# A language-model tower's front block: the embedding product moves two slots ahead and to the end of a step, the second-layer products next to the first, and ScalarE writes the rows of the second norm

## The reference, cut to what matters

```python
h = tok(x, emb_2, emb_3, emb_4)            # 64 x 256 tokens, 64 wide: three gathered rows, summed, / 4
h = h + attn(layernorm(h), k_w1, k_w2, q_w1, q_w2, v_w)
#   phase = tanh(tanh(x w1 + b1) w2 + b2) * pi, for keys and for queries (32 phases each)
#   out[t] = sum over t' <= t of (cos, sin)(key phase of t') . (cos, sin)(query phase of t) * value[t'] / norm[t]
h = h + experts(layernorm(h), edge_index)  # graph attention over 262,144 edges picks two of four experts
h = h + attn_of_heads(layernorm(h))
h = h + mlp_of_half_the_tokens(layernorm(h))
```

## Time and profile before

| what | us |
|---|---|
| median of 3 runs (lowest, highest) | 3619.52 (3614.86, 3619.73) |
| the profiled execution, its own time | 3614.07 |
| its span, first to last instruction | 3612.3 |
| VectorE busy in the span | 2905.8 |
| TensorE busy | 2745.7 |
| GpSimd busy | 2357.0 |
| ScalarE busy | 2233.4 |

### The profile page before, as it was taken

How to read it: one execution, slowest core, us unless ns; L and a number is a source line. 1 busy time by engine, 2 the same in 40 slices (tenths; PEclk the granted TensorE clock), 3 DMA queues, 4 the chain that set the end, 5 groups by cost and what they waited for, 6 DMA issues and landing times. The chain is left out here.

```text
span 3612.3 us, 65404 instructions
## 1 busy us (share of the span) xinstructions
PE 2745.7 (76%) x21085; PEld 2339.2 (65%) x21085; DVE 2905.8 (80%) x5994; ACT 2233.4 (62%) x3840; POOL 2357.0 (65%) x2290
## 2 busy tenths in 40 slices
PE   2556665649999999999999999999999500077747
PEld 1445554438888888888888888888888400054436
DVE  9988878847888888888888888888888857777764
ACT  2555545558787777777777777777777112255523
POOL 7887877027777777777777777777777577233311
PEclk8666667759999999999999999999999855566669
DMA  2111111012222222222222222222221132000002
GB/s 73 22 23 25 24 24 21 5 47 48 49 49 49 49 49 49 49 49 49 49 49 49 49 49 49 49 49 49 49 49 41 21 101 77 26 0 0 0 0 47
DMA packets 157459, 144.94 MB, mean 40 GB/s; under 512 B 71192, under 2 KB 133032, under 8 KB 156728
## 3 DMA queue, kind: packets, MB, share of 16 engines
q1 hardware_dynamic: 88608, 109.56, 9.1%
q0 software_dynamic: 68768, 34.45, 8.8%
HBM read 93.03 MB, written 50.82 MB: 40 GB/s over the span
## 5 line engine op out<-in xcount | busy, mean ns | idle before, releaser
L886 POOL DMA_INDIRECT es_got<-node_table,late x1632 | 1577.6, 967 | 497.3 <-issue 497.3
L966 PE MATMUL es_pgot<-hash_space,es_pick 128*128 128x256 bf16 x13056 | 1510.3, 277 | 16.4 <-ACT es_pick L904 16.4
L966 PEld LDWEIGHTS es_pgot<-hash_space,es_pick 128*128 128x128 bf16 x13056 | 1300.0, 100 | 182.6 <-issue 16.9
L900 ACT ACTIVATE es_pick<-es_away,consts 128x512 bf16<-128x512 f32 x1088 | 680.3, 712 | 7.0 <-DMA es_away<-sorted_keys 6.7
L348 POOL DMA_INDIRECT fr_ring<-in_emb,fr_rows x384 | 498.7, 1299 | 138.9 <-issue 115.8
L904 ACT ACTIVATE es_pick<-es_pick,consts 128x4096 bf16<-128x4096 bf16 x136 | 503.8, 3704 | 0.9
L1068 DVE TENSOR_TENSOR es_hot<-es_iota,late 128x1024 bf16<-128x1024 f32 x272 | 331.8, 1220 | 26.7 <-DVE es_st L1108 25.7
L1069 DVE TENSOR_TENSOR es_hot<-es_iota,late 128x1024 bf16<-128x1024 f32 x272 | 330.5, 1215 | 0.0
L1050 DVE TENSOR_REDUCE es_got<-es_prod 128x32 f32<-128x512 f32 x272 | 277.2, 1019 | 39.6
L1048 DVE TENSOR_TENSOR es_prod<-es_pgot,es_own 128x512 f32<-128x512 f32 x272 | 187.5, 689 | 123.4 <-PE es_pgot L966 86.2
L932 ACT ACT_TABLE_LOAD x64 | 82.1, 1283 | 301.2 <-PE ex_phid L973 301.2
(11 more groups left out here) (345 smaller groups left out, 4316.2 us busy)
## 6 DMA issues: line engine op xcount, KB each, us to landing
es_away<-sorted_keys SPq DMA_DIRECT2D x68, 512.0 KB
es_got<-node_table,late POOLq DMA_INDIRECT x1632
edge_states<-es_st SPq DMA_DIRECT2D x68, 384.0 KB, 2.4
expert_outputs<-ex_y SPq DMA_DIRECT2D x64, 256.0 KB
gt_y<-expert_outputs SPq DMA_DIRECT2D x8, 2048.0 KB, 8.6
fr_ring<-in_emb,fr_rows POOLq DMA_INDIRECT x384, 2.5
out_dram<-h SPq DMA_DIRECT2D x1, 4096.0 KB, 16.0
weights<-in_weights SPq DMA_DIRECT2D x1, 2110.0 KB, 14.0
```

The lines of the kernel that those rows point to most:

```text
L886: pool.indirect_dma_start(out=got[:, r, k, :], out_offset=None, in_=table_dram, in_offset=bass.IndirectOffsetOnAxis(ap=src[:, n, k:k + 1]. ...
L900: a.activation(pick[:, r, half, k], away[:, r, half * 4 * P:half * 4 * P + 4 * P], ACT.Square, bias=C("away")[:, k:k + 1]).then_inc(s_act, 1)
L966: mm = pe.matmul(p_got[:, q, c * 256:c * 256 + 256], pick[:, r, q // 2, k, at * P:at * P + P], parts[:, part, k], start=(k == 0 and part = ...
```

## The change

Five edits, all in `front`:

1. The embedding product is made two slots ahead, as the last thing of a step on TensorE (`embed(s + 2)`), and ScalarE evicts and squares it as the last thing of its step. Slot 1 is made in step 0.
2. The second-layer products (L774 before) follow the first-layer ones with only the table product and a possible turn between.
3. Of the second norm VectorE computes only the reciprocal and the product of mean and reciprocal (a 128 x 4 operation); ScalarE writes the four rows (an activation with scale and bias taken per partition).
4. Constants of placing: `turn_at` of the later parts of a step are called with t + 3.8 and t + 4.5 where they were t + 3.6, t + 4.2 and t + 5.0, and while a turn is under way, VectorE may pull a part forward by 1.3 exchanges where it was 0.8.
5. The last steps are fewer by one: slots 30 and 31 pass the second norm together.

```diff
--- before.py
+++ after.py
@@ -300,7 +300,12 @@
         PHASES = [("k", top) for top in range(1, 19)] + [("k", 18), ("t", 14)]
         final, final_top = (sum(range(1, 19)) + 1 + 18) % 2, 14 % 2
         is_slot = lambda s: 0 <= s < SLOTS
-        STEPS = SLOTS + 3
+        STEPS = SLOTS + 2
+
+        def lasts(s):
+
+            return [s - 3] if 3 <= s <= SLOTS else [SLOTS - 2, SLOTS - 1] if s == SLOTS + 1 else []
+
         top_dram = mem["top_dram"]
 
         stage = ExitStack()
@@ -381,13 +386,22 @@
             def root(s, ln):
                 a.activation(std[:, ln, slot(s)], var[:, ln, slot(s)], ACT.Sqrt, scale=1.0 / D, bias=C("eps")).then_inc((s_std0, s_std1)[ln], 1)
 
+            def normed(s, ln):
+
+                act.wait_ge((s_near0, s_near1)[ln], s + 1)
+                for t in range(ST):
+                    col = slice(s * ST + t, s * ST + t + 1)
+                    to = x1[:, t] if ln else x0[:, t % 2, t // 2]
+                    ins = a.activation(to, h[:, s * ST + t], ACT.Identity, scale=std[:, ln, col], bias=away[:, ln, col])
+                ins.then_inc((s_x0, s_x1)[ln], 1)
+
             evict(0)
             squares(0, 0)
             root(0, 0)
             one_set()
             act.wait_ge(s_weights, 16)
             for s in range(STEPS):
-                before, last = s - 1, s - 3
+                before = s - 1
                 if is_slot(before):
                     act.wait_ge(s_fold, before + 1)
 
@@ -395,28 +409,30 @@
                 if is_slot(s):
                     act.wait_ge(s_xt_p, s + 1)
                     a.activation(xt[:], p_xt, ACT.Copy).then_inc(s_xt, 1)
-                if is_slot(last):
+                for last in lasts(s):
+                    normed(last, 1)
                     act.wait_ge(s_x1_p, last + 1)
                     a.activation(xts[:, last * 2:last * 2 + 2], p_x1.rearrange("p (t n) -> p t n", t=2), ACT.Copy).then_inc(s_x1t, 1)
+                    if not is_slot(s):
+                        act.wait_ge(s_tab_p, last + 1)
+                        a.activation(tab[:, slot(last)], p_tab.rearrange("p (t r) -> p t r", r=ROW), ACT.Copy).then_inc(s_tab, 1)
                 if is_slot(s):
                     act.wait_ge(s_hid_p, s * 2 + 2)
                     for kq in range(2):
                         a.activation(hid[:, kq], p_hid[:, kq], ACT.Tanh, bias=W("q_b1" if kq else "k_b1")).then_inc(s_hid, 1)
-                if is_slot(s + 1):
-                    evict(s + 1)
-                    squares(s + 1, 0)
-                if is_slot(last):
-                    act.wait_ge(s_tab_p, last + 1)
-                    a.activation(tab[:, slot(last)], p_tab.rearrange("p (t r) -> p t r", r=ROW), ACT.Copy).then_inc(s_tab, 1)
-                if is_slot(s):
+                    for last in lasts(s):
+                        act.wait_ge(s_tab_p, last + 1)
+                        a.activation(tab[:, slot(last)], p_tab.rearrange("p (t r) -> p t r", r=ROW), ACT.Copy).then_inc(s_tab, 1)
                     act.wait_ge(s_ph, s * 2 + 2)
                     for kq in range(2):
                         a.activation(u[:, kq], p_ph[:, kq], ACT.Tanh, bias=W("q_b2" if kq else "k_b2")).then_inc(s_u, 1)
-                if is_slot(s + 1):
-                    root(s + 1, 0)
-                if is_slot(s - 2):
-                    root(s - 2, 1)
-                if is_slot(s):
+                    if s == 0:
+                        evict(1)
+                        squares(1, 0)
+                    if is_slot(s + 1):
+                        root(s + 1, 0)
+                    if is_slot(s - 2):
+                        root(s - 2, 1)
                     one_set()
                 if is_slot(before):
                     act.wait_ge(s_out, before + 1)
@@ -426,9 +442,15 @@
                             ins.then_inc(s_res, 1)
                     act.wait_ge(s_res, before + 1)
                     squares(before, 1)
+                if s == SLOTS:
+                    root(SLOTS - 2, 1)
+                    root(SLOTS - 1, 1)
                 if is_slot(s):
                     act.wait_ge(s_v, s + 1)
                     a.activation(val[:].rearrange("p two b d -> p (two b d)"), p_v, ACT.Copy).then_inc(s_val, 1)
+                if is_slot(s + 2):
+                    evict(s + 2)
+                    squares(s + 2, 0)
 
         @block.vector
         def _(dve):
@@ -487,11 +509,13 @@
 
                 dve.wait_ge((s_std0, s_std1)[ln], s + 1)
                 ch.step(v.reciprocal(std[:, ln, slot(s)], std[:, ln, slot(s)])); ch.settle()
-                for t in range(ST):
-                    col = slice(s * ST + t, s * ST + t + 1)
-                    to = x1[:, t] if ln else x0[:, t % 2, t // 2]
-                    ins = v.tensor_scalar(to, h[:, s * ST + t], away[:, ln, col], std[:, ln, col], ALU.add, ALU.mult)
-                ins.then_inc((s_x0, s_x1)[ln], 1)
+                if ln:
+                    v.tensor_tensor(away[:, ln, slot(s)], away[:, ln, slot(s)], std[:, ln, slot(s)], ALU.mult).then_inc(s_near1, 1)
+                else:
+                    for t in range(ST):
+                        col = slice(s * ST + t, s * ST + t + 1)
+                        ins = v.tensor_scalar(x0[:, t % 2, t // 2], h[:, s * ST + t], away[:, ln, col], std[:, ln, col], ALU.add, ALU.mult)
+                    ins.then_inc(s_x0, 1)
 
             def split(j):
 
@@ -510,8 +534,8 @@
                 if part == 0:
                     if is_slot(s):
                         normed(s, 0)
-                    if is_slot(s - 3):
-                        normed(s - 3, 1)
+                    for last in lasts(s):
+                        normed(last, 1)
                 if part == 1:
                     if is_slot(s - 1):
                         for b in range(SB):
@@ -559,7 +583,7 @@
                 turns[0] += 1
                 dve.sem_inc(s_turn_go, 1)
                 if arr == "k":
-                    between(done[0] + 0.8)
+                    between(done[0] + 1.3)
                 dve.wait_ge(s_turned, turns[0])
                 return turned[:, 0:COLS if arr == "k" else P]
 
@@ -656,7 +680,7 @@
                 s, part = divmod(at[0], 3)
                 attention(s, part)
                 at[0] += 1
-                if s >= SLOTS - 1 and ready < 3 and part != 1:
+                if s == SLOTS and part < 2:
                     prepare(ready)
                     ready += 1
             while ready < 3:
@@ -717,10 +741,18 @@
                                        ring[:, r, n].rearrange("p (b two) d -> p two b d", two=2)[:, half], start=(n == 0), stop=(n == 2))
                 mm.then_inc(s_emb, 1)
 
+            def table(s):
+
+                pe.wait_ge(s_x1t, s + 1)
+                pe.wait_ge(s_wx, 1)
+                for two in range(2):
+                    mm = pe.matmul(p_tab[:, two * 2 * ROW:two * 2 * ROW + 2 * ROW], xts[:, s * 2 + two], wx[:].rearrange("p two r -> p (two r)"), start=True, stop=True)
+                mm.then_inc(s_tab_p, 1)
+
             embed(0)
             pe.wait_ge(s_weights, 16)
             for s in range(STEPS):
-                before, last = s - 1, s - 3
+                before = s - 1
                 t = step_time(s)
                 turn_at(t + 0.1)
                 if is_slot(s):
@@ -737,15 +769,17 @@
                         k, q = (phi[b * D:b * D + D, kq] for kq in range(2))
                         pe.matmul(p_sc[b][:, 0:256], k[:, 0:P], q, start=True, stop=True)
                         pe.matmul(p_sc[b][:, 256:384], k[:, P:T], q[:, P:T], start=True, stop=True).then_inc(s_sc, 1)
-                if is_slot(last):
+                for last in lasts(s):
                     pe.wait_ge(s_x1, last + 1)
                     if is_slot(s):
                         pe.wait_ge(s_xt, s + 1)
-                    elif last >= 1:
+                    else:
                         pe.wait_ge(s_tab, last)
                     for two in range(2):
                         mm = pe.transpose(p_x1[:, two * P:two * P + P], x1[:, 2 * two:2 * two + 2].rearrange("p two d -> p (two d)"), ident)
                     mm.then_inc(s_x1_p, 1)
+                    if not is_slot(s):
+                        table(last)
                 if is_slot(before):
                     if before >= 1:
                         pe.wait_ge(s_res, before)
@@ -759,20 +793,15 @@
                     for kq in range(2):
                         pe.matmul(p_hid[:, kq], W("q_w1" if kq else "k_w1"), xt[:], start=True, stop=True).then_inc(s_hid_p, 1)
                 turn_at(t + 2.9)
-                if is_slot(s + 1):
-                    embed(s + 1)
-                if is_slot(last):
-                    pe.wait_ge(s_x1t, last + 1)
-                    pe.wait_ge(s_wx, 1)
-                    for two in range(2):
```

(13 more changed lines are left out.)

4 lines of the change are left out of this document (2 added, 2 removed).

## The result

The changed kernel took 3589.48 us, median of 5 runs (3585.23 to 3600.26), against 3617.19 for the kernel before in the same session: ratio 0.993, 95% interval 0.9918 to 0.9942. I had forecast 3613, no change that can be told, with 3595 as the lower end. The profiled execution took 3585.23 us, 28.8 less than the one before; my sum had 6.5 less.

What follows compares the result with a forecast made beforehand. VectorE's work or waiting was taken to bound the front after 222 us, with gathers alongside before. -16.6 - 41.5 + 15 + 30 + 5 + 1.6 = -6.5 us, so 3613 us as a median, range 3595 to 3627.

Steps and rivals of the forecast that it cites:

- There both walk together: First stretch, before 222 us: GpSimd's gathers (20.3 us a slot) and VectorE's seven steps (144.3 us) keep one pace.
- Rows of the second norm: Middle stretch: VectorE spared 0.72 us a step over 23 steps, -16.6 us; ScalarE's four rows, 1.1 us, cost nothing.
- Second layer: Middle stretch: VectorE's 35.0 us of waits for the second tanh and 6.5 for scores go, -41.5 us.
- ring: Dependence loop from mask through products, tanh, eviction, squares, sine and scores to mask: 18.3 us binds six short steps, +15 us.
- Turns and embedding product: Steps 8, 10 lose 7 and 5 us; 15, 27, 29 lose 16 together; with smaller terms, +30 us.
- Two slots ahead: First stretch: mask of slot 0 moves from 77.75 to 88.4, of slot 7 to 227; +5 us, bounds 0 and 8.
- the end: Last chain of the front: slots 30 and 31 add two writings of rows and drop some waiting, +1.6 us.
- Rival 1: The gain stays: faster TensorE, turns cost +12, ring 17 us and +7; -32 us, 3587. Chance 0.20.
- Rival 2: Slower by turns alone: slow TensorE after idling costs seven step-end turns 2 us more each, +14; 3627. Chance 0.15.
- Rival 3: The wait only moves: first-layer product held back 0.8 us, short steps cost 5 more; sum -1, 3618. Chance 0.20.

Runs made afterwards that it cites:

- the kernel with both parts: Kernel before plus ScalarE's second-norm rows and second-layer products next to the first, embedding product one slot ahead behind them: 3567.00 us, ratio 0.9858; disturbed 0.9967 and 0.9963.
- disturbed groups: Four of six groups of runs, in which TensorE paused with nothing to wait for and every kernel, the one before too, took 5260 to 5336 us.

## Why the prediction was wrong

Most of its mechanisms held. One did not, and left a part of the gain at nothing; several sizes were off as well. The sum was 22.4 us too high: 5.4 in the first stretch, 12.5 in the middle, 1.2 at the end, and 3.2 behind the front block, which the change doesn't touch.

**"There both walk together", the first stretch, is the step whose mechanism failed.** I took GpSimd's gathers as a limit beside VectorE and so counted neither the rows nor the second layer there, only the second slot's +5. The runs show -6.5 for the rows, -6.8 for the second layer, -11.6 for both (222.0 to 210.5), and +11.2 for the rest of the change. For the rows, the gathers gave way with VectorE's work: from the start of slot 3's to the end of slot 9's they took 141.5 us before and 133.9 with the rows on ScalarE. For the second layer they did not (140.5 us), and the seven steps were 6.8 us shorter all the same: before, the gathers were no limit any more by the end of the stretch. The last gather of slot 8 and the embedding product of slot 8, before:

```profile
197.23 0.94 POOL L348 DMA_INDIRECT fr_ring<-in_emb,fr_rows  x1 [0.30 <-issue]
...
201.80 2.04 PE L760 MATMUL fr_pb<-fr_xt,weights 128*128 128x256 f32 x4 [0.77 <-DVE fr_sm L519]
203.64 2.16 PE L716 MATMUL fr_turned<-fr_ring,consts 128*128 128x128 f32 x12
```

The product starts 5.4 us after the gather's end, behind a first-layer product that waited for the mask product; in slots 1 and 4, where it did wait for the gather, it was 1.6. With the second layer alone the slack is used up: the product waits for the gather in slots 5, 6, 7 and 9, in slot 7 so:

```profile
180.94 1.60 PE L715 MATMUL fr_turned<-fr_ring,consts 128*128 128x128 f32 x12 [0.41 <-DMA fr_ring<-in_emb,fr_rows]
```

Two errors of the stretch, 11.6 left out and 6.2 too little, leave 5.4. By size that is a quarter of the miss; the larger part, the 12.5 of the middle, is made of mis-sized terms. Worked out step by step from my terms, 3.4 of it lie in steps 8 and 9, 2.9 in steps 12, 16, 22, 25 and 28, some 2 in step 29, and the rest in portions of 1 us or less.

**Rows of the second norm, -16.6.** VectorE's own work fell by 18.7, 19.1 and 18.7 us in the middle in the three pairs of kernels that differ in it alone, 0.8 a step where I had 0.72, and by 4.9 in the first stretch, which I left out. The 128 x 4 operation, which I took at 0.17 us, costs 0.08 (in one step of the changed kernel it starts at 726.70, what follows at 726.78). The four rows take ScalarE 1.43 us (forecast 1.1, bound 1.2):

```profile
245.36 1.43 ACT L395 ACTIVATE fr_x<-h,fr_away,fr_std 128x64 f32<-128x64 f32 x4
```

They cost nothing that shows. By the Trainium skill (VectorE: DVE Perf Modes, the section on the TRN2 errata) an estimate was 0.45 a step; the measured 0.8 decides against it. The same section says that its table's row for VectorE comes out too short for a single operation and that the measured fixed term is about 150 cycles; an estimate from that is 0.22 us a row and 0.73 a step, close to what was measured. The section as a whole does not speak against the change.

**Second layer -41.5, ring +15.** Together -26.5; the kernel with this part alone gained 22.7 in the middle. The ring was forecast at 18.3 us; steps 12, 16, 22, 25 and 28 take 18.1, 17.4, 17.4, 18.3 and 17.4. In step 25, where TensorE's first-layer products take 2.05 us, it is 18.3 to the tenth; in the three of 17.4 they take 1.59, 1.92 and 1.18. Rows at the lower clock were taken for all steps, but the first-layer group took less than 2.0 us in 18 of 32 steps after and in 7 before, and the granted clock was 0.74 against 0.68. That the clock is the cause of the shorter ring is argued from these rows; no run set the clock alone.

**Turns and embedding product, +30.** Steps 15, 27 and 29 came as worked out: mask waits of 4.9, 5.4 and 5.5 us (forecast 4.7 to 5.9), 75.3 us in all. My terms give 78, because step 29 stands in two of them: in the ring with 2.4 and here with 5, where its mask product has one wait, 5.5 us. Step 8 waits 7.4 (27.7 us, forecast 29.2), step 10 takes 25.2 (25.3), step 11 23.6 (23.0), step 9 19.7 (21.6). The mechanism holds, the size is some 3 us high in steps 8 and 9.

**Two slots ahead, +5, and the end, +1.6.** The delay of the first mask was forecast to within 0.7 us. Catching up was under-estimated against the kernel before, since VectorE's shorter steps let it; against the best kernel one slot ahead the price is 11.2, double my figure. The end cost 0.5.

**The rivals.** Rival 1 gave 3587 and a ring near 17 us; it had the number, and about half of the reason. Its chance of 0.20, and a range that took in only its nearer half, were too small. The range's ends, 3595 and 3627, come from the turns (12 and 44) alone, not from the gathers too, as I wrote; with the gathers' 0 and 8 they are 3590 and 3630. Rival 2 named the slow turn: it is real (3.65 us after an idle TensorE, 1.94 behind work), but the turn waits of the changed kernel are only 1.1 us over those before. Rival 3 is refuted by the short steps of the changed kernel itself, none of which is over 18.3 us. None of them named what the runs found: the rest of the change takes back 22 us of the 52 that its two other parts give, and the second slot ahead is the likely cause.

## What to carry to other kernels

- Where two engines walk at one pace, ask whether the pace of the one depends on the other before taking it as a limit: gathers of 0.94 to 2.9 us took 141.5 us for seven slots and 133.9 when VectorE's work was cut. Ask too how long after its gather the product starts: 1.6 us where it waited for it, 5.4 where it didn't.
- A product that holds up a chain can be put behind it without being made a slot earlier: the first cost nothing, the second brought a gather wait at the start and, in steps 15, 27 and 29, a chain behind the turn. Undo the parts one by one, the best version may lie between the two kernels (3567, against 3619 and 3589).
- Tiles that share a PSUM buffer make an order of evictions: a place number in a table that lets a turn slip behind the values cost 9 us in one step. Putting turns first is no rule either: with two slots ahead it gave some 3 us in step 8 in two of three traces, and took 1.6 and 5 in steps 10 and 11.

## What the runs showed of the hardware

In the disturbed groups TensorE stood still with nothing waited for. TensorE in the kernel with both parts, in such a run, and at the same place undisturbed:

```profile
250.58 0.69 PE L742 MATMUL fr_pa<-consts,fr_x 128*128 128x128 f32 x2 [0.57 <-issue]
268.10 0.79 PE L749 MATMUL fr_pb<-fr_phi 64*128 64x256 f32 x1 [16.84 <-issue]
```
```profile
251.25 0.69 PE L742 MATMUL fr_pa<-consts,fr_x 128*128 128x128 f32 x2 [2.54 <-DVE fr_x L504]
254.50 0.79 PE L749 MATMUL fr_pb<-fr_phi 64*128 64x256 f32 x1 [2.56 <-ACT fr_phi L403]
```

The products themselves take the same 0.79 us. In the stream of edges behind the front the page has, for the 13056 products of one line, first disturbed, then undisturbed:

```profile
L977 PE MATMUL es_pgot<-hash_space,es_pick 128*128 128x256 bf16 x13056 | 1834.1, 288 | 1427.7 <-issue 1407.4
```
```profile
L977 PE MATMUL es_pgot<-hash_space,es_pick 128*128 128x256 bf16 x13056 | 1513.0, 277 | 16.7 <-ACT es_pick L915 16.7
```

A product lasts 288 ns in place of 277, but 109 ns lie idle ahead of each. The same chip ran the kernel before at 3619 us in one group and at 5291 in the next; what brings it about no run here shows. The changed kernel itself was never run in that condition.
